# A macaron block on one core: quartered gate, down products by tokens, row statistics and additions moved to GpSimd

## The chip, the cores and the metric

One core of a Trainium2 chip runs the whole program. Its engines are TensorE (PE), VectorE (DVE), ScalarE (ACT), GpSimd (POOL) and SyncE (SP, which only issues DMAs). Times are device microseconds of one execution; a kernel's time is the median of its runs.

## The reference

For 4096 tokens x of 128 features (8 sequences of 512), all in float32 but the experts' products:

```python
x = x + 0.5 * ffn(layernorm(x))
x = x + attention(layernorm(x))   # one head, 4096 stored keys and values, softmax
x = x + 0.5 * ffn(layernorm(x))   # the same weights again

def ffn(x):                       # 8 experts of 176 hidden units, the best 2 of each token
    scores = sigmoid(x @ gate_w.T)
    _, sel = top_k(scores + expert_bias, 2)
    # routed: x * score in bfloat16, up, relu squared, down, summed over the two experts
    hs = square(relu(x @ shared_w_up.T))
    return routed + hs @ shared_w_down.T
```

## The kernel before

Tokens are handled in 8 groups of 512 (4 tiles of 128). `G` counts groups over both FFNs: 0 to 7 in the first, 8 to 15 in the second. Each engine has its own program, written out by hand; engines wait for one another on semaphores, and within an engine everything runs in the order written. So the order of calls in each `ffn(f)` is the schedule.

An FFN group goes like this. GpSimd computes the inverse deviation and normalises (L469, L483), TensorE transposes x to features by tokens (L1211), ScalarE copies it out of PSUM (L640) and GpSimd casts it to bfloat16 (L506). This runs three groups ahead. The gate (L1217) multiplies each tile of x, as the stationary operand, by the 8 columns of gate weights, so the logits stand by tokens. ScalarE takes exponentials (L648). `route_group(k, G)` (L973) is the routing of one group, or from group 2 on of two at once, in 16 small steps on VectorE: sigmoid, bias, twice a highest value with a tie broken by rank, sum of the two choices (k = 14), product with the score (k = 15). GpSimd spreads each weight over 16 rows (L495), TensorE transposes that (L1238) and ScalarE copies it (L671) to `wbc`, which holds for each hidden row and token the weight of its expert.

All experts are computed for all tokens: the hidden units, 8 x 176 = 1408, are 11 chunks of 128 rows. `up(G, k)` (L1255) makes two chunks (k = 5: one) of hidden rows by 512 tokens, VectorE multiplies relu by `wbc` (`relu_weighted`, L1028), ScalarE squares (L665), and `down(G, k)` (L1275) sums the chunks' products in one PSUM bank, features by tokens. The shared expert runs in float32: L1227 up, L656 relu, L660 square, L1289 down, added in the same bank. ScalarE copies the bank to `yT` (L676), TensorE transposes it back to tokens by features (L1247), and VectorE adds half of it to X (`residual`, L1043). The down products of slots 3 to 5 of a group are done within the next one.

```python
                    if i + 1 < GROUPS:
                        pe.wait_ge(xT_copied, min(n + AHEAD + 1, 2 * base + GROUPS))
                        if f == 0 and i + AHEAD >= GROUPS:
                            pe.wait_ge(xT_copied, GROUPS + 1)
                        transpose_weights(G + 1, xT_bank)
                    down(G, 1)
                    up(G, 4)
                    up(G, 5)
                    shared_down(G)
                    down(G, 2)
```

Layer norms are numbered n, 24 in all. For n from 4 to 8 VectorE takes only the raw statistics and GpSimd joins the halves of a row (`join_halves`, L447); for the others VectorE aggregates them (L914). During the first FFN GpSimd also splits the keys and values into two parts (L543 to L552). The attention lies between the FFNs; in its last steps it already normalises groups 8 to 10 and computes their gates (`early_gate`, L1480). SyncE stores each finished group (L428).

## Time and profile before

| | us |
|---|---|
| median of 3 runs (lowest to highest) | 642.77 (642.2 to 643.43) |
| the profiled execution | 644.01 |
| its span, first to last instruction | 642.2 |
| busy: TensorE, VectorE, ScalarE, GpSimd | 609.9, 531.3, 456.1, 398.9 |
| granted TensorE clock, mean over the span | 0.997 of 2.4 GHz |

The profile lists what each engine did. Busy time of matmuls is modelled: each one is shown until its result is out, and neighbours overlap, so the distance from start to start tells what one costs. "PEld" is the load of the stationary operand, which runs beside the products. The time slices tell where in the program the time lies: the first FFN ends at about 100 us, the second begins at 552.7.

### The profile page before, as it was taken

What the parts mean: (1) busy time and instruction counts of PE and PEld (TensorE: products, weight loads), DVE (VectorE), ACT (ScalarE), POOL (GpSimd) and SP (SyncE); (2) the same over time, 40 slices, a digit from 0 to 9 for tenths busy, and PEclk for the clock granted to TensorE, in tenths of its full rate; (3) what the DMA queues carried; (4) which work ended last, traced back from release to release, by engine and by line L of the source; (5) the groups of instructions that cost most, each with busy time, mean ns of one, the idle gap of its engine ahead of it and who ended that gap; (6) DMA issues with size and microseconds to landing.
All of it is one profiled execution on the core that took longest, in us unless ns stands there. A gap on an engine that the chain in (4) does not pass through costs nothing.

```text
span 642.2 us, 9438 instructions
## 1 busy us (share of the span) xinstructions
PE 609.9 (95%) x2884; PEld 430.1 (67%) x2884; DVE 531.3 (83%) x944; ACT 456.1 (71%) x765; POOL 398.9 (62%) x443
## 2 busy tenths in 40 slices
PE   7799999799999999999999999999999998999997
PEld 4455445567677787777777777777777766645543
DVE  5889887998987978978988897897898858699885
ACT  3577787566677767778777777777776775667886
POOL 4987770564486875966867777586687786524000
PEclk9899999999999999999999999999999999999999
DMA  8011210435447365374553835727355350000000
GB/s 313 6 57 42 65 34 1 114 74 131 113 96 170 73 152 113 85 173 91 132 126 79 177 85 126 152 59 178 82 121 130 77 123 1 2 17 17 34 33 33
DMA packets 36113, 59.19 MB, mean 92 GB/s; under 512 B 9312, under 2 KB 9952, under 8 KB 35936
## 3 DMA queue, kind: packets, MB, share of 16 engines
q1 hardware_dynamic: 31808, 52.82, 34.2%
q10 hardware_dynamic: 3744, 4.73, 2.9%
q0 software_dynamic: 512, 1.05, 0.6%
q8 instruction: 23, 0.38, 0.3%
q14 instruction: 26, 0.21, 0.1%
HBM read 8.23 MB, written 2.10 MB: 16 GB/s over the span
## 4 chain that ended last, share of the span: by engine, by line
PE 60%; DVE 24%; issue 5%; SPq 4%; ACT 3%; POOL 2%; DMA 1%; ACTq 0%; DVEq 0%; POOLq 0%
PE banks L1425 6%; PE banks L1427 6%; PE banks L1426 6%; PE banks L1466 6%; PE banks L1468 6%; PE banks L1467 6%; DVE bank_max L1143 6%; DVE E L1138 5%; PE banks L1281 4%; SPq L356 4%; PE banks L1272 4%; PE banks L1445 4%; DVE probsT L1039 4%; PE banks L1476 2%; DVE p_lo L1131 2%
## 5 line engine op out<-in xcount | busy, mean ns | idle before, releaser
L559 POOL TENSOR_TENSOR p_lo<-probsT,p_hi 128x768 fp32r<-128x768 f32 (+1 forms) x128 | 227.0, 1777 | 120.5 <-ACT p_hi L770 119.9
L1143 DVE TENSOR_REDUCE bank_max<-banks 128x1 f32<-128x1024 f32 x128 | 155.9, 1218 | 29.8 <-PE banks L1427 29.0
L770 ACT ACTIVATE p_hi<-probsT 128x768 fp32r<-128x768 f32 (+1 forms) x128 | 104.3, 816 | 27.7 <-PE banks L1468 22.8
L1425 PE MATMUL banks<-kv_lo,q_parts 128*128 128x512 f32 x256 | 111.5, 436 | 4.6 <-ACT E L795 1.7
L1138 DVE STREAM_TRANSPOSE E<-E 128x1024 f32<-128x1024 f32 x92 | 113.5, 1234 | 0.9 <-ACT E L795 0.9
L1039 DVE SCALAR_TENSOR_TENSOR probsT<-banks,E 128x1024 bf16<-128x1024 f32 x80 | 95.3, 1217 | 21.4 <-PE banks L1272 21.3
L669 ACT ACTIVATE probsT<-probsT 128x1024 bf16<-128x1024 bf16 x96 | 92.6, 982 | 23.2 <-DVE probsT L1039 18.7
L795 ACT ACTIVATE E<-banks,neg_max 128x1024 f32<-128x1024 f32 x92 | 102.4, 1113 | 8.6 <-DVE neg_max L1149 5.6
L1466 PE MATMUL banks<-p_hi,kv_lo 128*128 128x512 f32 x256 | 107.7, 421 | 0.3 <-issue 0.3
L1467 PE MATMUL banks<-p_lo,kv_hi 128*128 128x512 f32 x256 | 102.3, 400 | 0.0
L1468 PE MATMUL banks<-p_hi,kv_hi 128*128 128x512 f32 x256 | 102.2, 399 | 0.0
L1427 PE MATMUL banks<-kv_hi,q_parts 128*128 128x512 f32 x256 | 101.2, 396 | 0.0
L1426 PE MATMUL banks<-kv_hi,q_parts 128*128 128x512 f32 x256 | 101.1, 395 | 0.0
L754 ACT ACTIVATE p_hi<-banks 128x256 fp32r<-128x256 f32 (+1 forms) x128 | 52.2, 408 | 61.5 <-PE banks L1445 61.4
L1131 DVE TENSOR_TENSOR p_lo<-banks,p_hi 128x256 fp32r<-128x256 f32 (+1 forms) x128 | 56.1, 439 | 30.9 <-ACT p_hi L754 30.4
L1425 PEld LDWEIGHTS banks<-kv_lo,q_parts 128*128 128x128 f32 x256 | 48.2, 188 | 13.3 <-ACT E L795 3.1
L1466 PEld LDWEIGHTS banks<-p_hi,kv_lo 128*128 128x128 f32 x256 | 48.2, 188 | 12.5 <-issue 2.5
L1468 PEld LDWEIGHTS banks<-p_hi,kv_hi 128*128 128x128 f32 x256 | 48.1, 188 | 12.3
L1467 PEld LDWEIGHTS banks<-p_lo,kv_hi 128*128 128x128 f32 x256 | 48.2, 188 | 11.6 <-issue 1.7
L1427 PEld LDWEIGHTS banks<-kv_hi,q_parts 128*128 128x128 f32 x256 | 48.1, 188 | 11.2
L1272 PE MATMUL banks<-E,wup_b 128*128 128x512 bf16 x176 | 51.1, 384 | 4.3 <-DVE probsT L1039 3.0
L1445 PE MATMUL banks<-ident,probs 128*128 128x128 f32 x256 | 51.5, 276 | 3.3 <-DVE p_lo L1131 1.7
(132 smaller groups left out, 895.6 us busy)
## 6 DMA issues: line engine op xcount, KB each, us to landing
probsT<-E SPq DMA_DIRECT2D x208, 128.0 KB, 2.4
probsT<-E SPq DMA_DIRECT2D x232, 64.0 KB, 2.0
probsT<-E ACTq DMA_DIRECT2D x72, 64.0 KB, 2.3
E<-in_keys_values SPq DMA_DIRECT2D x8, 512.0 KB, 3.6
out<-X SPq DMA_DIRECT2D x8, 256.0 KB, 2.1
X<-in_x SPq DMA_DIRECT2D x1, 1280.0 KB, 8.8
probsT<-E POOLq DMA_DIRECT2D x16, 64.0 KB, 2.3
X<-in_x SPq DMA_DIRECT2D x3, 256.0 KB, 5.2
```

What stands on the lines that cost most here:

```text
L559: pool.tensor_tensor(moved_part(p_lo, ring), moved_pair(ring // UP, ring % UP), moved_part(p_hi, ring).bitcast(fp32), ALU.subtract).then_i ...
L770: act.activation(moved_part(p_hi, ring), moved_pair(ring // UP, ring % UP), ACT.Copy).then_inc(moved_hi_done, 1)
L795: act.activation(strips[:, 2 * h * QUADS:2 * (h + 1) * QUADS, :, :], source.rearrange("p k (c b q) -> p (k c) b q", b=QUADS, q=SQ), ACT.Ex ...
L1039: dve.scalar_tensor_tensor(hidden[:, k, :, :], up_banks[PAIR_BANK[k]], 0.0, spread.unsqueeze(1).to_broadcast([P, 2, N]), ALU.max, ALU.mult ...
L1138: dve.transpose(half, half).then_inc(squares_done, 1)
L1143: dve.tensor_reduce(bank_max[:, i % 2, h:h + 1], score_pair(u, i, h).rearrange("p b n -> p (b n)"), AX.X, ALU.max).then_inc(bank_max_done, 1)
L1425: pe.matmul(bank, qh, kl, start=True, stop=False)
L1426: pe.matmul(bank, ql, kh, start=False, stop=False)
L1427: pe.matmul(bank, qh, kh, start=False, stop=True).then_inc(scores_done, 1)
L1466: pe.matmul(OB, vl, hi, start=(c == 0), stop=False)
L1467: pe.matmul(OB, vh, lo, start=False, stop=False)
L1468: pe.matmul(OB, vh, hi, start=False, stop=(c == KC - 1)).then_inc(pv_done, 1)
```

## The change

- The gate's operands are swapped: the gate weights, padded to 32 columns, are stationary, and x moves. The four tiles go to the four column quarters of the array (`tile_position`), and the logits come out as rows 32t to 32t+7 by tokens. ScalarE takes exponentials of all 128 rows, and VectorE turns them with a transpose of 32x32 blocks before the routing. Tokens are thereby in another order, which the copy to `wbc` undoes.
- Routing: `STEPS` is 14; the last two operations are counted apart. In groups G + 1 = 2, 4, 6, 10, 12, 14 GpSimd does them, ahead of spreading the weights, and that stands before the row statistics now. On VectorE steps 0 to 5 stand in the even group (before: 0 to 8), 6 to 9 before `relu_weighted(G, 1)` and 10 to 13 behind it.
- Down and shared down: the hidden block is the stationary operand, 128 tokens at a time, and the weights move, so the result stands by tokens. `yT`, `copy_yT` and `transpose_back` go. Two result banks alternate.
- The transpose of the spread weights stands behind the shared down product.
- Second FFN: for n of 20 to 23 GpSimd joins the statistics; for groups 8 to 14 ScalarE copies half of the result to `half_result` and GpSimd adds it to X. Group 15 and the first FFN keep VectorE's addition, now straight from the result bank.

The core of the diff (declarations and semaphores that only follow are left out):

```diff
 RING = AHEAD + 1
-STEPS = 15
+STEPS = 14
 LOWEST = -3.0e38
...
 def joins_on_pool(n):
-    return AHEAD < n <= ATTENTION_LN
+    return AHEAD < n <= ATTENTION_LN or n > SECOND_LN + AHEAD
...
     return sum(not joins_on_pool(k) for k in range(n))
+def added_on_pool(G):
+    return GROUPS <= G < 2 * GROUPS - 1
+def added_before(G):
+    return sum(added_on_pool(k) for k in range(G))
...
         xT = [xq[:, :]] + [probs[:, 0, 0, c * N:(c + 1) * N] for c in range(AHEAD)]
+        expz_rows = probs[:, 0, 0, AHEAD * N:AHEAD * N + 2 * P].rearrange("p (s n) -> p s n", s=2)
+        expz = probs[:, 0, 0, AHEAD * N + 2 * P:].rearrange("p (s t e) -> p s t e", s=2, t=GT)
+        early_rows = wq_scaled[:, :]
         probsT = sb("probsT", [P, 2, MOVED * QUADS, KC, SQ], fp32)
...
         up_banks = [banks[:, 0:2, :], banks[:, 2:4, :]]
-        y_bank, z_bank, gate_bank, xT_bank = (banks[:, 4 + b, :] for b in range(4))
+        result_banks = [banks[:, 4 + b, :] for b in range(2)]
+        gate_bank, xT_bank = (banks[:, 6 + b, :] for b in range(2))
         TB, OB = banks[:, 2 * SCORE_PAIRS, :], banks[:, 2 * SCORE_PAIRS + 1, :]
...
+        def finishes_on_pool(G):
+            return G >= 2 and route_event(G) != route_event(GROUPS)
+        def routing(G):
+            T = GT * (2 if G >= 2 else 1)
+            return tuple(route[:, a, 0:T, :] for a in range(6))
         def wide_weights(G):
...
             for g in range(GROUPS):
-                sp.wait_ge(x_updated, GROUPS + g + 1)
+                if added_on_pool(GROUPS + g):
+                    sp.wait_ge(x_added, added_before(GROUPS + g + 1))
+                else:
+                    sp.wait_ge(x_updated, updated_before(2 * GROUPS))
                 sp.dma_start(out[:, tiles_of(g), :], X[:, tiles_of(g), :]).then_inc(stored, 16)
...
                 T = (slots.stop - slots.start) * GT
+                if finishes_on_pool(G):
+                    event = route_event(G)
+                    score, _, hit, _, first, second = routing(G)
+                    pool.wait_ge(route_step, STEPS * (event + 1))
+                    pool.tensor_tensor(hit, first, second, ALU.add).then_inc(route_summed, 1)
+                    pool.wait_ge(route_summed, event + 1)
+                    pool.wait_ge(weights_spread, event)
+                    pool.tensor_tensor(weight[:, slots, :, :].rearrange("p s t e -> p (s t) e"), hit, score, ALU.mult
+                                       ).then_inc(weights_ready, 1)
                 pool.wait_ge(weights_ready, route_event(G) + 1)
...
                                  .to_broadcast([P, T * E, ROWS])).then_inc(weights_spread, 1)
+            def add_result(G):
+                pool.wait_ge(result_copied, added_before(G + 1))
+                xg = X[:, tiles_of(G % GROUPS), :].rearrange("p t d -> p (t d)")
+                pool.tensor_tensor(xg, xg, half_result, ALU.add).then_inc(x_added, 1)
...
                     next_ln = i + AHEAD + 1
+                    if i % 2 == 1 and i + 1 < GROUPS:
+                        spread_weights(G + 1)
                     if next_ln < GROUPS + (1 - f):
...
                         spread_weights(1)
-                    if i % 2 == 1 and i + 1 < GROUPS:
-                        spread_weights(G + 1)
                     if i + AHEAD < GROUPS:
...
                         normalize(n + AHEAD + 1, next_ln % GROUPS)
+                    if i and added_on_pool(G - 1):
+                        add_result(G - 1)
                     if f == 0:
...
                 if G >= 2:
-                    act.wait_ge(route_step, STEPS * route_event(G - 2) + 1)
-                act.activation(expz[:, G % 2, :, :].rearrange("p t e -> p (t e)"), logits, ACT.Exp, scale=-1.0
-                               ).then_inc(expz_done, 1)
+                    act.wait_ge(expz_turned, route_event(G - 2) + 1)
+                act.activation(early_rows if G == GROUPS else expz_rows[:, G % 2, :], logits, ACT.Exp, scale=-1.0).then_inc(expz_done, 1)
...
                 wait(act, weighted, (G - 1) * SLOTS)
-                act.activation(wbc[:, G % 2, :], bank, ACT.Copy).then_inc(wbc_copied, 1)
-            def copy_yT(G):
+                act.activation(wbc[:, G % 2, :].rearrange("p (t a q) -> p t a q", t=GT, a=GT),
+                               bank.rearrange("p (a t q) -> p t a q", a=GT, t=GT), ACT.Copy).then_inc(wbc_copied, 1)
+            def copy_result(G):
                 act.wait_ge(down_done, (G + 1) * SLOTS)
-                wait(act, z_done, G)
-                act.activation(yT[:, :], y_bank[:, :], ACT.Copy).then_inc(yT_copied, 1)
+                wait(act, x_added, added_before(G))
+                act.activation(half_result, result_banks[G % 2], ACT.Copy, scale=0.5).then_inc(result_copied, 1)
...
                     cast_up()
-                    exp_logits(0, gate_bank[:, 0:GT * E])
+                    exp_logits(0, gate_bank[:, 0:P])
                     copy_xT(1, 1, 1, xT_bank)
                     cast_down()
-                    exp_logits(1, gate_bank[:, 0:GT * E])
+                    exp_logits(1, gate_bank[:, 0:P])
                     scale_q_weights()
...
                     if i + AHEAD < GROUPS:
-                        exp_logits(G + AHEAD, gate_bank[:, 0:GT * E])
+                        exp_logits(G + AHEAD, gate_bank[:, 0:P])
                     elif f == 0 and i + AHEAD == GROUPS:
...
                     square(G, 2)
+                    square(G, 3)
                     if i + 1 < GROUPS:
                         copy_wbc(G + 1, xT_bank)
-                    square(G, 3)
                 square(base + GROUPS - 1, PAIRS - 1)
                 square(base + GROUPS - 1, PAIRS)
-                copy_yT(base + GROUPS - 1)
...
                 T = (slots.stop - slots.start) * GT
-                score, biased, hit, tagged, first, second = (route[:, a, 0:T, :] for a in range(6))
+                score, biased, hit, tagged, first, second = routing(G)
                 top, first_tag, top2, second_tag = (best[:, a, 0:T] for a in range(4))
...
                 biases = ebias[:, :].unsqueeze(1).to_broadcast([P, T, E])
-                logits = expz[:, slots, :, :].rearrange("p s t e -> p (s t) e")
+                logits = expz[:, slots, :, 0:E].rearrange("p s t e -> p (s t) e")
                 weights = weight[:, slots, :, :].rearrange("p s t e -> p (s t) e")
...
                 if k == 0:
+                    dve.wait_ge(expz_done, G + (2 if T > GT else 1))
+                    wait(dve, route_step, STEPS * (event - 1) + 1)
+                    turned = expz[:, slots, :, :].rearrange("p s t e -> p (s t e)")
+                    if G == GROUPS:
+                        dve.transpose(turned[:, 0:P], early_rows)
+                        dve.transpose(turned[:, P:], expz_rows[:, 1, :]).then_inc(expz_turned, 1)
+                    else:
+                        dve.transpose(turned, expz_rows[:, slots, :].rearrange("p s n -> p (s n)")
+                                      ).then_inc(expz_turned, 1)
                     wait(dve, weights_ready, event)
-                    dve.wait_ge(expz_done, G + (2 if T > GT else 1))
-                else:
+                    dve.wait_ge(expz_turned, event + 1)
+                elif k <= STEPS:
                     dve.wait_ge(route_step, event * STEPS + k)
...
                 elif k == 14:
-                    dve.tensor_tensor(hit, first, second, ALU.add).then_inc(route_step, 1)
+                    dve.tensor_tensor(hit, first, second, ALU.add).then_inc(route_summed, 1)
                 else:
+                    dve.wait_ge(route_summed, event + 1)
                     wait(dve, weights_spread, event)
...
-                dve.wait_ge(z_done, G + 1)
+                dve.wait_ge(down_done, (G + 1) * SLOTS)
                 xg = X[:, tiles_of(g), :].rearrange("p t d -> p (t d)")
-                dve.scalar_tensor_tensor(xg, z_bank[:, :], 0.5, xg, ALU.mult, ALU.add).then_inc(x_updated, 1)
+                dve.scalar_tensor_tensor(xg, result_banks[G % 2], 0.5, xg, ALU.mult, ALU.add).then_inc(x_updated, 1)
...
                             dve.wait_ge(consts_set, 1)
-                            for k in range(STEPS + 1):
+                            for k in range(STEPS + 2):
                                 route_group(k, 0)
...
                     relu_weighted(G, 0)
+                    routes = i % 2 == 1 and i + 1 < GROUPS
+                    if routes:
+                        for k in range(6, 10):
+                            route_group(k, G + 1)
+                        relu_weighted(G, 1)
+                        for k in range(10, STEPS):
+                            route_group(k, G + 1)
                     if ahead < GROUPS + (1 - f):
                         moments_of(n + AHEAD + 1, ahead % GROUPS)
-                    if i % 2 == 1 and i + 1 < GROUPS:
-                        for k in range(9, STEPS + 1):
-                            route_group(k, G + 1)
                     if f == 0 and i == 0:
-                        for k in range(STEPS + 1):
+                        for k in range(STEPS + 2):
                             route_group(k, 1)
-                    relu_weighted(G, 1)
+                    if not routes:
+                        relu_weighted(G, 1)
                     relu_weighted(G, 2)
-                    if i:
+                    if i and not added_on_pool(G - 1):
                         residual(G - 1, i - 1)
...
                     if i % 2 == 0 and i + 2 < GROUPS:
-                        for k in range(0, 5):
+                        for k in range(0, 3):
                             route_group(k, G + 2)
...
                     if i % 2 == 0 and i + 2 < GROUPS:
-                        for k in range(5, 9):
+                        for k in range(3, 6):
                             route_group(k, G + 2)
...
+            def gate_products(bank, xt):
+                for t in range(GT):
+                    last = pe.matmul(bank[t * SQ:(t + 1) * SQ, :], gate_s[:, :], xt[:, t * P:(t + 1) * P], start=True,
+                                     stop=True, tile_position=(0, t * SQ))
+                last.then_inc(logits_done, 1)
             def gate(n, G):
...
                 wait(pe, weighted, (G - AHEAD) * SLOTS)
-                for t in range(GT):
-                    last = pe.matmul(gate_bank[:, t * E:(t + 1) * E], xT[G % RING][:, t * P:(t + 1) * P], gate_s[:, :],
-                                     start=True, stop=True)
-                last.then_inc(logits_done, 1)
+                gate_products(gate_bank[:, 0:P], xT[G % RING])
...
                 last.then_inc(wbc_done, 1)
-            def transpose_back(G):
-                pe.wait_ge(yT_copied, G + 1)
-                wait(pe, x_updated, G)
-                for t in range(GT):
-                    last = pe.transpose(z_bank[:, t * D:(t + 1) * D], yT[:, t * P:(t + 1) * P], ident[:, :])
-                last.then_inc(z_done, 1)
...
                 if k == 0:
-                    wait(pe, yT_copied, G)
+                    if G >= 2 and added_on_pool(G - 2):
+                        pe.wait_ge(result_copied, added_before(G - 1))
+                    elif G >= 2:
+                        pe.wait_ge(x_updated, updated_before(G - 1))
                 chunks = (2 * k,) if k == PAIRS else (2 * k, 2 * k + 1)
                 for c in chunks:
-                    last = pe.matmul(y_bank[:, :], wdown_b[:, c, :], hidden[:, k, c % 2, :], start=(c == 0),
-                                     stop=(c == CH - 1))
+                    for t in range(GT):
+                        last = pe.matmul(result_banks[G % 2][:, t * D:(t + 1) * D],
+                                         hidden[:, k, c % 2, t * P:(t + 1) * P], wdown_b[:, c, :],
+                                         start=(c == 0 and t == 0), stop=(c == CH - 1 and t == GT - 1))
                 last.then_inc(down_done, 1)
...
-                pe.matmul(z_bank[:, 0:columns], ident[:, :], ones[:, 0:columns], start=True, stop=True)
+                pe.matmul(result_banks[1][:, 0:columns], ident[:, :], ones[:, 0:columns], start=True, stop=True)
...
                 pe.wait_ge(hs_done, G + 1)
-                pe.matmul(y_bank[:, :], sdown_s[:, 0, :], hs[:, 0:N], start=False, stop=False)
-                for c in range(2):
-                    pe.matmul(y_bank[:, c * HALF:(c + 1) * HALF], sdown_s[:, 1 + c, :], hs[:, N:], start=False,
+                for t in range(GT):
+                    tokens = result_banks[G % 2][:, t * D:(t + 1) * D]
+                    pe.matmul(tokens, hs[:, t * P:(t + 1) * P], sdown_s[:, 0, :], start=False, stop=False)
+                    at_column = N + t * P % HALF
+                    pe.matmul(tokens, hs[:, at_column:at_column + P], sdown_s[:, 1 + t * P // HALF, :], start=False,
                               stop=False)
...
                         up(G, 2)
-                        if i:
-                            transpose_back(G - 1)
                         down(G, 0)
...
                         up(G, 3)
+                    down(G, 1)
+                    up(G, 4)
+                    up(G, 5)
+                    shared_down(G)
                     if i + 1 < GROUPS:
...
                         transpose_weights(G + 1, xT_bank)
-                    down(G, 1)
-                    up(G, 4)
-                    up(G, 5)
-                    shared_down(G)
                     down(G, 2)
...
                     scores(0, 1, 0)
-                transpose_back(base + GROUPS - 1)
```

## Rows read from the trace of the kernel before

**Rows 1.** The page: busy time by engine, and the chain by engine.
```profile
PE 609.9 (95%) x2884; PEld 430.1 (67%) x2884; DVE 531.3 (83%) x944; ACT 456.1 (71%) x765; POOL 398.9 (62%) x443
...
PE 60%; DVE 24%; issue 5%; SPq 4%; ACT 3%; POOL 2%; DMA 1%; ACTq 0%; DVEq 0%; POOLq 0%
```

**Rows 2.** Time slices, one per group: busy us by engine, granted clock, DMA share, GB/s.
```profile
33.90:44.20 10.30, 10.30 (x55) 5.86 (x54) 9.37 (x20) 8.87 (x13) 7.97 (x18) 1.00 0.16 51
...
54.80:66.70 11.90, 11.05 (x55) 6.08 (x56) 10.87 (x24) 9.86 (x14) 8.11 (x18) 1.00 0.15 44
...
564.00:575.90 11.90, 10.95 (x55) 6.06 (x56) 11.12 (x29) 9.56 (x14) 4.68 (x9) 1.00 0.06 23
575.90:586.20 10.30, 10.30 (x55) 5.92 (x54) 9.17 (x23) 7.83 (x12) 3.70 (x8) 1.00 0.07 27
...
627.50:642.20 14.70, 10.17 (x44) 4.29 (x42) 7.52 (x8) 8.59 (x11) 0.00 (x0) 0.99 0.09 36
```

**Rows 3.** Timeline of TensorE, group 10: start, length of the run, line, count.
```profile
575.87 1.02 PE L1230 MATMUL banks<-probs,sup_s 128*128 128x512 f32 x2
576.82 0.65 PE L1233 MATMUL banks<-probs,sup_s 128*64 128x256 f32 x4
577.40 0.82 PE L1281 MATMUL banks<-probsT,wdown_b 128*128 128x512 bf16 x3
...
579.36 0.60 PE L1252 MATMUL banks<-ident,probsT 128*128 128x128 f32 x4
...
580.34 1.06 PE L1223 MATMUL banks<-gate_s,probs 128*128 128x8 f32 x8
581.26 0.59 PE L1272 MATMUL banks<-E,wup_b 128*128 128x512 bf16 x2
...
583.20 1.02 PE L1291 MATMUL banks<-probsT,sdown_s 128*128 128x512 f32 x2
584.06 1.03 PE L1294 MATMUL banks<-probsT,sdown_s 128*128 128x256 f32 x4
```

**Rows 4.** Weight loads and short pairs: line L1281, two loads in a timeline, a run of L1476.
```profile
L1281 PEld LDWEIGHTS banks<-probsT,wdown_b x176: 95/98/151, 23.8 to 637.2; 128*128 128x128 bf16 x176
...
577.40 0.11 PEld L1281 LDWEIGHTS banks<-probsT,wdown_b 128*128 128x128 bf16 x2 [0.39 <-issue]
...
555.11 1.05 PE L1476 MATMUL banks<-wo_s,attended 128*128 128x128 f32 x8
```

**Rows 5.** Waits, 33.9 to 99.2 us, then 564 to 642.2 us: total, times, longest.
```profile
DVE probsT L1039 <- PE banks L1272: 6.7, 9, 1.8
...
DVE probsT L1039 <- PE banks L1272: 8.4, 10, 1.8
```

**Rows 6.** VectorE: line L1138, and groups of instructions from 564 to 607.9 us.
```profile
L1138 DVE STREAM_TRANSPOSE E<-E x92: 1224/1234/1248, 114.9 to 510.3; 128x1024 f32<-128x1024 f32 x92
...
L1047 DVE SCALAR_TENSOR_TENSOR X<-banks,X 128x512 f32<-128x512 f32 x4 | 2.7, 681 | 0.0
...
L921 DVE BATCH_NORM_AGGREGATE moments<-stats 128x2 f32<-128x6 f32 x12 | 1.1, 156 | 0.1
```

**Rows 7.** GpSimd's addition L580 by itself; a routing step on VectorE beside GpSimd's work.
```profile
L580 POOL TENSOR_TENSOR X<-X,attended x14: 1269/1288/1296, 180.3 to 536.9; 128x512 f32<-128x512 f32 x14
...
543.45 1.26 DVE L1022 TENSOR_TENSOR route<-route 128x64 f32<-128x64 f32 x1
```

**Rows 8.** Group 0: timelines of TensorE and VectorE with idle time, and a time slice.
```profile
27.84 1.09 PE L1244 MATMUL banks<-ident,probsT 128*128 128x128 f32 x4 [1.54 <-issue]
...
30.67 1.23 DVE L1039 SCALAR_TENSOR_TENSOR probsT<-banks,E 128x1024 bf16<-128x1024 f32 x1 [1.37 <-PE banks L1272]
...
28.00:29.00 1.00, 1.00 (x5) 0.81 (x5) 0.90 (x4) 0.04 (x1) 1.00 (x3) 0.50 0.00 0
```

**Rows 9.** The end: timeline of ScalarE's last copy and VectorE's last addition.
```profile
637.66 0.60 ACT L679 ACTIVATE probsT<-banks 128x512 f32<-128x512 f32 x1 [0.48 <-PE banks L1281]
...
639.00 0.69 DVE L1047 SCALAR_TENSOR_TENSOR X<-banks,X 128x512 f32<-128x512 f32 x1 [2.84 <-PE banks L1252]
```

39 lines of the change are left out of this document (19 added, 20 removed).

## The prediction

> **What bounds the kernel now.** I read the page first. TensorE is busy 95% of the span and the chain that ended last runs 60% through it, 24% through VectorE [rows 1]. Matmul ends are modelled, so I then took the time slices from one group of 512 tokens to the next, cut where the shared product of each group starts [rows 2]. In both FFNs a group without the second half of the routing takes about 10.3 us, one with it 11.9 us. In the first kind TensorE has no gap; in the second VectorE is busy 10.9 to 11.1 of 11.9 us and TensorE idles nearly 1 us. The attention between the FFNs (some 100 to 550 us) is not edited, apart from three gate products at its end. So the time is to be won in 16 groups, at the start and at the tail.
>
> The TensorE timeline of one group [rows 3] gives the price list, by start to start: down product with 512 moving columns 0.216 us; transposing back 4 tiles 0.43 (4 x 0.109); gate 580.34 to 581.26 = 0.92; shared down product 0.86 for L1291 (583.20 to 584.06) and as much for L1294. The waits [rows 5] say that the two engines hold each other up by turns: VectorE waited 6.7 us for up products in the first FFN and 8.4 us in the second.
>
> **The change, part by part.**
>
> *Down products by tokens.* The hidden block becomes the stationary operand, 128 tokens at a time, so 11 pairs of load and product with 512 columns become 44 pairs with 128. Before: 11 x 0.216 = 2.37 us. The unknown is the spacing p of a bf16 pair with 128 columns; no such pair is in the trace. Lower bound: a quarter of a 512-column product, 0.054 us. Upper bound: the fp32 pair with 128 columns, 0.111 us ((1.05 - 0.275)/7 in the row of L1476 [rows 4]), where the 0.19 us load counts. The bf16 load is recorded at 0.098 us and two of them start about 0.013 us apart (0.11 - 0.098) [rows 4]; the product that needs the load starts right behind it. A load that another can follow after 0.013 us should hide behind 0.054 us of columns, so I take p = 0.056: 44 x 0.056 = 2.46, **+0.09 us** a group. The range keeps 0.054 to 0.111.
>
> *Shared down product by tokens.* 16 fp32 pairs with 128 columns at 0.111 = 1.78 instead of 2 x 0.86 = 1.72: **+0.06**.
>
> *Transposing back.* It goes: **-0.43** on TensorE. ScalarE's copy before it (0.60 us, L679 [rows 9]) goes in the first FFN and stays as copy_result in the second, but is no longer on TensorE's way, since two result banks alternate.
>
> *Quartered gate.* 32 stationary columns per tile, four tiles in the four column quarters of the array, logits by rows. The nearest row is the half product L1233: two tiles of 256 columns [rows 3]. It starts 0.95 us after L1230, whose two passes take 0.85, so 0.10 to change over; and it gives way after 0.58 where its columns alone need 0.43 if the halves run together, so 0.15 to change back. For the gate: 0.10 + 0.21 + 0.15 = 0.46, **-0.45** after rounding. If the quarters don't run together: 0.25 + 4 x 0.21 = 1.1, +0.18.
>
> TensorE's sum: 0.09 + 0.06 - 0.43 - 0.45 = **-0.73 us** for a group with a gate, **-0.28** without one.
>
> *VectorE.* Each routing now transposes the exponentials first: the 128x1024 transpose takes 1.23 us [rows 6], a quarter of it about 0.31, with issue 0.35 per pair of groups. In the first FFN nothing is taken off in return but two closing steps of 0.23 of each later routing. So there a pair of groups is -0.1 us for VectorE, no gain. In the second FFN seven residual additions of 0.68 go to GpSimd, and four aggregations (1.1 us over three groups, with the memset 0.4 each) [rows 6]: 4.8 + 1.6 = 6.4 us off. The order "6 to 9, relu, 10 to 13" only moves steps, it puts relu and weighting of slot 1 ahead of four of them: nothing, or a little gain for ScalarE's next square.
>
> *GpSimd.* It takes 7 additions of the form of L580, 1.29 us each [rows 7], the joins and two small operations per routing, in a stretch where it is idle over half the time [rows 2]. They hide; if they don't, the stores are late, and only the last one is on the path, whose addition VectorE does. Two waits are new on its queue. Spreading the weights now stands ahead of the statistics and waits for VectorE's steps up to 13 with one relu between them, about 1.2 + 1.0 + 1.2 + 1.0 = 4.4 us into the group; behind it stand join, cast, normalisation and the key conversion. All of that was 8.1 us in such a group [rows 2], plus 0.5 for the two new operations: 13.0, and the normalised x is transposed some 2.5 us into the next group, at 14. It fits, in the first FFN by 1 us only, so there GpSimd is the next to be late.
>
> *ScalarE.* Eight copies of 0.60 less in the first FFN, exponentials over 128x128 instead of 128x32, a regrouped copy of the weights. Off the path. In the second FFN copy_result waits until GpSimd has added the result before; behind that wait stand all squares of the group, and so the down products. The addition before was due a whole group earlier, so I cost the wait at nothing. TensorE's first down product waits for the result of two groups ago where it waited for the copy of one: looser.
>
> *Moved weights transpose.* It now stands behind the shared down product. At the start this matters: TensorE stood still for 1.54 us before L1244 in group 0, in the slice that follows the granted clock is 0.50 (the 1.2 GHz level) against 1.00 elsewhere, and VectorE then waited 1.37 us for an up product [rows 8]. With the transpose behind them, slots 4 and 5 and the shared product fill that hole. I count VectorE's 1.37 and some of what the lower clock cost: **-1.7**. Elsewhere the weights are needed 2 to 3 us later than they are ready: nothing.
>
> *Tail.* Before, the last down product is followed by copy (637.66), transposes and the addition at 639.00 [rows 9]. The addition can now start at 637.66: **-1.35**.
>
> **The sum.** First FFN: the start -1.7; four intervals in which TensorE has no gap, three at 0.73 and the last without gate at 0.28, -2.5; two with VectorE as the limit, -0.2 each, -0.4; the last transposing back, -0.4: together -5.0. Second FFN: first group -0.3; two intervals with routing, where TensorE gives 0.73 and VectorE over 0.9, -0.8 each; two without, -0.73 each; two late ones without gate, -0.35 each; the last group -0.28 and the tail -1.35: together -5.7. Gates at the end of attention: three times 0.45, half of it in waits, -0.7. Total **-11.4 us**. The profiled execution took 644.0 us (span 642.2): 632.6. The median of the runs is 642.8, 1.2 lower, so I forecast **631.4**.
>
> **The rivals.**
>
> *Pairs bound by the load* (slower than before). Place: the 44 pairs of each group, 704 in all, on an engine without gaps. Each 0.010 us more costs 7 us. The gain of 11.4 is used up at p = 0.056 + 11.4/704 = 0.072. At the fp32 spacing of 0.111 it would be +39 - 11 = +27, about 670. For it speaks that every 128-column pair in the trace runs at 0.108 to 0.112; against it that those are fp32 loads of 0.14 to 0.19 us, and bf16 loads follow one another after 0.013. Chance 0.09.
> The Trainium skill, "TensorE: Matmul & The Clock Gate", section "Back-to-back issue gap", speaks against the change here: it has a sustained stream of load and product pairs at about 81 ns for 128 columns and about 131 ns for 512. By it the sum would be an estimated 704 x 0.025 = 17.6 us worse, some 649. The trace contradicts its second figure, since pairs with 512 columns stand at 216 ns here, and the same section gives an isolated gap of about 56 ns; so I give it a part of the 0.09.
>
> *VectorE becomes the limit and keeps most of it.* In the first FFN it already fills 10.9 of 11.9 us in every second group, and if the other groups only hand their 0.73 over to longer waits of TensorE, what is left is start, tail and the second FFN in part: -1.7 - 1.35 - 3 = -6, about 637. Added to it can be contention: a routing step of 0.23 us took 1.26 beside GpSimd's work (L1022 at 543.45) [rows 7]; with GpSimd's additions in three routings that is up to 3 us. Chance 0.15.
> The Trainium skill, "SBUF — State Buffer", section "Who interferes with whom", has the reason: an operation of VectorE with two inputs in SBUF and one of GpSimd that reads SBUF exclude each other for a whole instruction. The trace agrees with that row.
>
> *The quarters don't run together.* Then 0.63 is missing in some nine groups that TensorE bounds, about 5.5 us: 637. Against it: the two halves of L1233 do. Chance 0.06.
>
> *More than forecast.* VectorE's waits for up products (6.7 and 8.4 us [rows 5]) shrink with TensorE's time in the groups with routing too, and square follows relu sooner. Then 0.5 more in each of six groups and 1 to 2 at the start: 627. Chance 0.15.
>
> **The numbers.** The forecast has 0.55, from 629 to 634. What a measurement of this kernel can tell from no change is about 0.2%, 1.3 us. All cases but the first end below that: faster 0.87, with 0.04 within 0.2% for a p near 0.072 or for several small losses together, slower 0.09. The range for 8 in 10 reaches from 626 to 638: it takes in both cases around 637 and the one at 627, and leaves the loads out.
>
> **What would show it.** Pairs of down products in the changed trace at 0.056 us start to start (at 0.08 or more the forecast is wrong); the gate in about 0.46 us with its four tiles starting nearly together; groups in the second FFN of 9.6 us without routing and about 11 with; in the first FFN 9.6 and 11.7; no stop of 1.5 us before the first weights transpose, and a granted clock without a slice at 0.50 or with a shorter one; the last addition right behind the last down product. It would be wrong in its mechanism if TensorE now waits for VectorE for longer than it gained, or if attention changes by more than 1 us.

## The result, and the profile after

The changed kernel takes 640.2 us (median of 7 runs, 638.77 to 641.1), the kernel before 643.75 in the same session (7 runs). The ratio is 0.9941, 95% interval 0.9922 to 0.9961: 3.8 us faster, a third of the 11.4 that were forecast, and outside the range. The profiled execution is the median one: 640.2, span 638.4 against 642.2.

The page after, busy time by engine (compare [rows 1]):

```profile
PE 597.5 (94%) x3508; PEld 443.3 (69%) x3508; DVE 525.7 (82%) x915; ACT 455.0 (71%) x756; POOL 414.7 (65%) x482
```

TensorE lost 12.4 us of busy time and VectorE 5.6, but the span only 3.8. Where it went is seen by cutting both traces at the same places: the shared up product of group 0, of 7, of 8 and of 15. Time slices of the kernel before (columns as in [rows 2]):

```profile
16.70:98.80 82.10, 76.28 (x372) 41.20 (x371) 71.29 (x143) 60.49 (x84) 64.43 (x125) 0.98 0.13 39
98.80:553.10 454.30, 439.23 (x2072) 338.82 (x2071) 378.75 (x610) 323.05 (x583) 309.17 (x253) 1.00 0.47 107
553.10:627.50 74.40, 71.21 (x356) 38.78 (x356) 65.02 (x137) 58.44 (x81) 18.44 (x36) 1.00 0.06 22
```

and of the changed one, which has the last group as well (before: 14.70 [rows 2]):

```profile
16.90:97.50 80.60, 71.15 (x640) 47.47 (x638) 71.49 (x141) 58.77 (x77) 66.20 (x131) 1.00 0.13 41
97.50:551.00 453.50, 437.64 (x2118) 338.20 (x2116) 377.41 (x612) 322.67 (x582) 308.84 (x253) 1.00 0.45 107
551.00:625.30 74.30, 68.27 (x625) 46.24 (x624) 60.85 (x108) 59.49 (x80) 31.72 (x68) 1.00 0.06 23
625.30:638.40 13.10, 8.96 (x90) 6.14 (x87) 6.95 (x7) 8.39 (x11) 1.27 (x1) 1.00 0.11 40
```

Groups 0 to 6 gave 1.5 us, the last group of the first FFN with the attention 0.8, the last group with the tail 1.6; the second FFN's groups 8 to 14 gave 0.1, though TensorE lost 2.9 us of work there and VectorE 4.2. Slices by group (those of [rows 2], but for the last):

```profile
31.70:42.90 11.20, 9.88 (x97) 6.79 (x95) 10.44 (x22) 8.46 (x12) 7.95 (x19) 1.00 0.16 48
52.90:65.20 12.30, 10.29 (x97) 6.88 (x94) 11.47 (x24) 9.05 (x12) 8.96 (x20) 1.00 0.14 44
561.70:573.10 11.40, 10.09 (x94) 6.79 (x94) 9.97 (x23) 9.43 (x13) 5.60 (x15) 1.00 0.01 2
573.10:583.30 10.20, 9.87 (x96) 6.67 (x93) 8.51 (x14) 8.06 (x12) 7.82 (x17) 1.00 0.14 54
```

Group by group, from the start of one shared up product to that of the next, in us (the forecast is the prediction's sum, spread over its groups; groups 1, 3, 5, 9, 11 and 13 hold the second half of a routing; groups 7 and 15 end in the stretches above):

| group | before | forecast change | after | measured change |
|---|---|---|---|---|
| 0 | 17.21 | -1.7 | 14.83 | -2.38 |
| 1 | 10.35 | -0.73 | 11.22 | +0.87 |
| 2 | 10.60 | -0.73 | 9.95 | -0.65 |
| 3 | 11.81 | -0.2 | 12.30 | +0.49 |
| 4 | 10.60 | -0.73 | 9.94 | -0.66 |
| 5 | 12.13 | -0.2 | 12.42 | +0.29 |
| 6 | 9.40 | -0.28 | 9.92 | +0.52 |
| 8 | 10.92 | -0.3 | 10.65 | -0.27 |
| 9 | 11.82 | -0.8 | 11.42 | -0.40 |
| 10 | 10.35 | -0.73 | 10.24 | -0.11 |
| 11 | 11.37 | -0.8 | 11.42 | +0.05 |
| 12 | 10.35 | -0.73 | 10.18 | -0.17 |
| 13 | 10.19 | -0.35 | 10.43 | +0.24 |
| 14 | 9.39 | -0.35 | 9.92 | +0.53 |

So groups 1 to 6 together are 0.9 us slower than before, where 2.9 faster were forecast. But that sum hides two opposite things: groups 2 and 4 gave nearly all that was forecast for them, and the groups beside them took it back.

TensorE's timeline of group 10 (compare [rows 3]) shows that the prices were right:

```profile
573.10 1.08 PE L1296 MATMUL banks<-probs,sup_s 128*128 128x512 f32 x2
...
574.69 0.84 PE L1345 MATMUL banks<-wdown_b,probsT 128*128 128x128 bf16 x12
575.37 0.59 PE L1330 MATMUL banks<-E,wup_b 128*128 128x512 bf16 x2
...
577.17 0.62 PE L1345 MATMUL banks<-wdown_b,probsT 128*128 128x128 bf16 x8 [0.34 <-ACT probsT L716]
577.72 0.43 PE L1282 MATMUL banks<-probs,gate_s 128*32 128x128 f32 x8
578.08 0.61 PE L1330 MATMUL banks<-E,wup_b 128*128 128x512 bf16 x2
...
579.73 0.38 PE L1358 MATMUL banks<-sdown_s,probsT 128*128 128x128 f32 x2
...
581.51 0.60 PE L1310 MATMUL banks<-ident,probsT 128*128 128x128 f32 x4
581.95 0.61 PE L1345 MATMUL banks<-wdown_b,probsT 128*128 128x128 bf16 x8
582.39 0.59 PE L1330 MATMUL banks<-E,wup_b 128*128 128x512 bf16 x2
```

Twelve down pairs take 0.68 us (574.69 to 575.37) and eight 0.44 (581.95 to 582.39): 0.056 a pair. The quartered gate takes 0.36 (577.72 to 578.08), the shared down product 1.78 (579.73 to 581.51). What has grown is the wait in brackets, of TensorE for the square. In the kernel before it came to 1.6 us in the first FFN (33.9 to 99.2 us) and in the second (564 to 642.2 us) to:

```profile
PEld banks L1281 <- ACT probsT L669: 4.5, 10, 0.7
```

In the changed kernel, first from 31.7 to 97.5 us, then from 561.7 to 638.4:

```profile
PEld banks L1345 <- ACT probsT L716: 7.4, 14, 1.0
...
DVE probsT L1096 <- PE banks L1330: 7.1, 7, 1.9
```

```profile
DVE probsT L1096 <- PE banks L1330: 12.9, 11, 1.9
...
PEld banks L1345 <- ACT probsT L716: 10.9, 15, 1.3
```

VectorE's waits for up products, 6.7 and 8.4 us before [rows 5], grew too. Both engines have less to do and each waits more for the other.

The tail did what was forecast. Timelines of TensorE and VectorE:

```profile
633.79 1.39 PE L1345 MATMUL banks<-wdown_b,probsT 128*128 128x128 bf16 x22
```

```profile
635.22 0.69 DVE L1104 SCALAR_TENSOR_TENSOR X<-banks,X 128x512 f32<-128x512 f32 x1 [1.74 <-PE banks L1345]
```

The addition follows the last down product directly; before, copy and transposes stood between [rows 9].

### The profile page after: what moved, and what is told of

Same layout as the page of the kernel before. It is cut to its first block, busy times and chain, and to the rows that moved or that the text cites. A ratio compares the mean times of both kernels' runs of the same rounds, so it can differ in the third digit from the quotient of the medians.

```text
span 638.4 us, 10666 instructions
## 1 busy us (share of the span) xinstructions
PE 597.5 (94%) x3508; PEld 443.3 (69%) x3508; DVE 525.7 (82%) x915; ACT 455.0 (71%) x756; POOL 414.7 (65%) x482
## 3 DMA queue, kind: packets, MB, share of 16 engines
q0 software_dynamic: 512, 1.05, 0.6%
## 4 chain that ended last, share of the span: by engine, by line
PE 65%; DVE 24%; issue 4%; ACT 3%; SPq 1%; DMA 1%; POOL 1%; ACTq 0%; DVEq 0%; POOLq 0%
PE banks L1488 8%; PE banks L1489 7%; PE banks L1490 7%; PE banks L1529 7%; PE banks L1531 7%; PE banks L1530 7%; DVE probsT L1096 6%; PE banks L1508 4%; DVE bank_max L1205 4%; PE banks L1345 4%; DVE E L1200 3%; PE banks L1330 3%; PE banks L1539 2%; PE banks L1361 2%; PE banks L1358 2%
## 5 line engine op out<-in xcount | busy, mean ns | idle before, releaser
L716 ACT ACTIVATE probsT<-probsT 128x1024 bf16<-128x1024 bf16 x96 | 92.4, 981 | 16.7 <-DVE probsT L1096 12.4
L1345 PEld LDWEIGHTS banks<-wdown_b,probsT 128*128 128x128 bf16 x704 | 42.5, 98 | 30.8 <-ACT probsT L716 21.7
L1345 PE MATMUL banks<-wdown_b,probsT 128*128 128x128 bf16 x704 | 52.8, 220 | 7.9 <-ACT probsT L716 7.9
```

What stands on the lines that cost most here:

```text
L1345: last = pe.matmul(result_banks[G % 2][:, t * D:(t + 1) * D], hidden[:, k, c % 2, t * P:(t + 1) * P], wdown_b[:, c, :], start=(c == 0 and ...
```

## The experiments

Every run was timed together with the kernel before, in one session. "Interiors" are the profiled distances from the shared up product of group 0 to that of 7, and of 8 to 15. Between two profiles of similar kernels the stretch between (attention) differs by up to 2 us, so I read the interiors for mechanisms and the ratio for the total. A group that an edit doesn't touch mostly repeats from profile to profile within 0.05 us.

| run | median us | ratio (95% interval) | interiors |
|---|---|---|---|
| before | 643.75 | | 82.1, 74.4 |
| the change | 640.2 | 0.9941 (0.9922 to 0.9961) | 80.6, 74.3 |
| e1_weights_before_up4 | 640.61 | 0.9952 (0.994 to 0.9963) | 80.6, 75.2 |
| e2_up1_first | 639.71 | 0.9938 (0.9926 to 0.995) | 80.1, 75.1 |
| e3_weights_and_up1 | 640.18 | 0.9946 (0.9934 to 0.9958) | 79.9, 75.8 |
| e7_gate_as_before | 639.82 | 0.994 (0.9925 to 0.9956) | 79.1, 74.5 |
| e5_vector_adds | 639.1 | 0.9938 (0.9923 to 0.9953) | 80.5, 73.5 |
| e4_before_weights_late | 654.57 | 1.017 (1.0152 to 1.0188) | 86.1, 81.6 |
| e4b_..._square_first | 648.24 | 1.0068 (1.0045 to 1.0092) | 82.4, 79.4 |
| g0_before_first_late | 644.0 | 0.9999 (0.999 to 1.0008) | 80.2, 74.4 |
| i1_first_early | 641.55 | 0.9977 (0.9964 to 0.999) | 81.5, 74.2 |
| f2_routing_and_weights_as_before | 650.09 | 1.011 (1.0082 to 1.0137) | 85.3, 77.1 |
| f3_split_as_before_weights_early | 642.63 | 0.9981 (0.9972 to 0.9991) | 83.0, 74.0 |
| h1_less_shared_down | 635.51 | 0.9874 (0.9862 to 0.9887) | 79.7, 72.9 |
| h2_less_vector | 637.19 | 0.9901 (0.9887 to 0.9916) | 79.6, 72.0 |
| h3_both_less | 630.12 | 0.9798 (0.9785 to 0.9811) | 76.9, 69.3 |
| i2_early_where_ready | 639.21 | 0.9933 (0.9921 to 0.9944) | 80.1, 73.8 |
| i3_..._vector_adds | 638.14 | 0.9918 (0.9906 to 0.9931) | 80.1, 73.0 |
| j1_best | 638.28 | 0.9914 (0.9897 to 0.9931) | 80.4, 73.0 |

### Is TensorE's work still the bound? The gate put back

The changed kernel with the old gate (tiles of x stationary, 0.92 us instead of 0.45). There the exponentials of group 8 stand in a part of the attention's buffer for exponentials that is still in use, so a part of the attention's result is overwritten; the work is the same.

```diff
-                    last = pe.matmul(bank[t * SQ:(t + 1) * SQ, :], gate_s[:, :], xt[:, t * P:(t + 1) * P], start=True,
-                                     stop=True, tile_position=(0, t * SQ))
+                    last = pe.matmul(bank[:, t * E:(t + 1) * E], xt[:, t * P:(t + 1) * P], gate_s[:, 0:E], start=True,
+                                     stop=True)
```

> The changed kernel with the gate as before: x stationary, eight moving columns, exponentials over 128x32, no transpose of them on VectorE. TensorE has 0.47 us more for each gate again. Loop theory: the gate stands where TensorE is ahead of VectorE, so its saving was never on the path, while the transpose of the exponentials on VectorE (0.44 us) is, in each pair of groups: 0 to 2.5 us less than the changed kernel. Theory of the prediction, TensorE without gaps in the groups without routing: 4 us or more slower than the changed kernel.

In total nothing changed: 639.82, ratio 0.994. But the edit does two things at once. TensorE has 0.47 us more per gate, and VectorE is rid of the transpose of the exponentials (0.44 us per routing). By group they come apart. A slice of group 10, which took 10.24 us in the changed kernel:

```profile
571.60:582.10 10.50, 10.17 (x96) 7.54 (x94) 8.41 (x14) 8.38 (x13) 7.77 (x17) 1.00 0.14 52
```

Groups 10 and 12 are 0.30 and 0.36 us longer with the old gate, so there most of the gate's saving had arrived; groups 3, 5, 8 and 11 are 0.2 to 0.35 us shorter. Group 0 is 0.9 us shorter but starts 0.9 us later (17.75 against 16.89). So the quartered gate together with the transpose that it needs was worth nothing; its saving on TensorE by itself was worth something in two groups, and for groups 2 and 4, unchanged within 0.05 us, this run can't part the two.

### Who keeps the square late in the second FFN? VectorE's additions back

```diff
 def added_on_pool(G):
-    return GROUPS <= G < 2 * GROUPS - 1
+    return False
...
```

> The changed kernel with VectorE's additions in the second FFN too (no result copies on ScalarE, no additions on GpSimd). Loop theory: of two additions of 0.68 us one lies in VectorE's stretch of the loop and the other where VectorE is ahead; against it a routing step that took 0.90 instead of 0.19 us beside GpSimd's addition is short again. Within 1 us of the changed kernel. Theory of the prediction, VectorE limits by its sum: 0.68 us more in each of seven groups, 4 to 5 us slower. Theory of ScalarE's queue: 1 to 2 us faster, as the square of slot 0 no longer stands behind the copy.

Seven additions of 0.68 us came back to VectorE, and by the ratio the time is the same (0.9938 against 0.9941); the second interior is 73.5 instead of 74.3. So giving the additions away, with the copy on ScalarE that this needs, gained nothing, and the copy costs. The ScalarE timeline of the changed kernel, group 10:

```profile
574.80 0.81 ACT L705 ACTIVATE probsT<-banks 128x768 f32<-128x768 f32 x1 [0.77 <-PE banks L1299]
575.57 0.60 ACT L728 ACTIVATE probsT<-banks 128x512 f32<-128x512 f32 x1
576.07 1.05 ACT L716 ACTIVATE probsT<-probsT 128x1024 bf16<-128x1024 bf16 x1
```

The shared relu (L705) waits for the shared up product, then comes copy_result (L728), then the first square (L716), and TensorE's down product starts at 577.17, 4.07 us after the shared up product. Before, the distance was much the same, 3.99 us, but TensorE's own work filled it, transposing back last (from 575.87 to 579.86, with transposing back at 579.36 [rows 3]). Taking 0.43 us of that work away leaves the chain as long as it was. Without the copy (the run with VectorE's additions, ScalarE and then TensorE) the square follows the relu and the down product comes 3.57 us after its shared up product at 572.44; groups 10 and 12 are 0.29 and 0.23 us shorter for it:

```profile
574.15 0.81 ACT L705 ACTIVATE probsT<-banks 128x768 f32<-128x768 f32 x1 [0.77 <-PE banks L1299]
574.86 1.05 ACT L716 ACTIVATE probsT<-probsT 128x1024 bf16<-128x1024 bf16 x1
```

```profile
572.44 1.08 PE L1296 MATMUL banks<-probs,sup_s 128*128 128x512 f32 x2
...
576.01 0.61 PE L1345 MATMUL banks<-wdown_b,probsT 128*128 128x128 bf16 x8
```

### Is it the hand-over between the engines? Order on TensorE

Three orders of the changed kernel: the weights transpose ahead of the up product of slot 4, where TensorE waits 1.05 us in groups with routing; the up product of slot 1 ahead of the last two down products of the group before; and both. In groups 0 and 8 the transpose stays where it is. The edit in short, without its waits:

```diff
 down(G, 1)
+transpose_weights(G + 1, xT_bank)      # e1, e3
 up(G, 4)
 up(G, 5)
 shared_down(G)
-transpose_weights(G + 1, xT_bank)
```

> The changed kernel, with the transpose of the spread weights between the first half of the down products and up(G, 4) instead of behind the shared down product (group 0 keeps it). Same work, another place. Theory of the hand-over: the interior of the FFNs gained nothing because what stands on TensorE between up(G, 5) and up(G+1, 0), up(G+1, 1) is what VectorE waits for at every group's start (0.56 to 1.16 us before slot 0, 1.15 to 1.93 before slot 1), and the change put 0.44 us of weights transpose exactly there. Then VectorE's idle time before slot 0 or 1 falls by about 0.4 us in some eight groups, and the time by 2.5 to 3.5 us against the changed kernel (to 0.989 to 0.990 of the kernel before). Theory that the two engines are filled with work, or that later routing weights set the pace: no change within 0.5 us, or slower by up to 1.5 us because TensorE then stands before up(G, 4) until the weights are there.

> The changed kernel, with up(G, 1) ahead of the last two down products of the group before (0.67 us of TensorE) instead of behind them. Same work. Hand-over theory: VectorE's wait before slot 1 (1.15 us in the even groups, 1.93 in the late ones) shrinks by about 0.6 us in seven groups: 3 to 4.5 us less than the changed kernel. Work theory: nothing. A third theory, ScalarE's squares as the limit: slower, as the result of the group before is taken off later and the square of slot 0 stands behind that in the second FFN.

> Both moves of the two kernels above together. Hand-over theory: the gains add up as long as VectorE has idle time before slots 0 and 1: 5.5 to 8 us less than the changed kernel, about 633 us where the changed kernel takes 640. If another chain (square, GpSimd) follows closely, clearly less than the sum of both.

None gained (ratios 0.9952, 0.9938, 0.9946). The first order fails by what is ready when. GpSimd and TensorE in group 11 of the changed kernel:

```profile
588.68 0.33 POOL L535 TENSOR_TENSOR route<-route 128x64 f32<-128x64 f32 x1 [7.42 <-DVE route L1045]
...
589.47 1.04 POOL L543 COPY probsT<-weight 128x1024 f32<-128x1024 f32 x1
```

```profile
590.56 0.82 PE L1330 MATMUL banks<-E,wup_b 128*128 128x512 bf16 x3 [1.05 <-DVE probsT L1096]
```

The weights are spread at 590.51, just when slot 2 sets the up product free, so the transpose can't use that hole; and it made group 13 longer (11.3 against 10.4 us): there TensorE stood 1.14 us ahead of the transpose, and the up product of slot 4 went out behind it.

### The late transpose by itself, and the start

The kernel before, with nothing but the transpose behind the shared down product; then the same with the square of slot 3 ahead of the copy to `wbc`, as the change has it; then only in groups 0 and 8; and last the changed kernel with these two groups as before.

```diff
-transpose_weights(G + 1, xT_bank)
 down(G, 1)
 up(G, 4)
 up(G, 5)
 shared_down(G)
+transpose_weights(G + 1, xT_bank)
 down(G, 2)
```

> The kernel before, with only the place of the weights transpose changed as the change does it: behind the shared down product. Hand-over theory: the start gains 1.5 to 2.4 us (the hole before the first transpose and the half clock behind it go), and groups that VectorE then waits for at their start lose 0.4 us each, seven to ten of them: 3 to 4 us lost, in all 1 to 2 us slower than the kernel before or the same. If the place doesn't matter in the interior: 1.5 to 2.4 us faster.

> The kernel before, with the weights transpose behind the shared down product and, as in the change, ScalarE's copy of the weights behind the square of slot 3 instead of ahead of it. The kernel that moved the transpose alone lost 10.9 us, its groups ending in a wait of 0.93 us for that square. Theory: 2.2 us gained at the start, 0.44 us lost in each group whose transpose stands in the loop, nine or so: 1 to 3 us slower than the kernel before. If the loss of the first kernel was the place of the transpose and not the square behind the copy: still some 10 us slower.

Alone, the move costs 10.9 us (1.017). ScalarE's copy waits for the transpose, and the square of slot 3 stands behind it. ScalarE, then TensorE's down product of slot 3:

```profile
591.16 0.60 ACT L674 ACTIVATE E<-banks 128x512 f32<-128x512 f32 x1 [2.13 <-PE banks L1244]
...
591.66 1.99 ACT L669 ACTIVATE probsT<-probsT 128x1024 bf16<-128x1024 bf16 x2
...
592.76 0.60 PE L1281 MATMUL banks<-probsT,wdown_b 128*128 128x512 bf16 x2 [0.77 <-ACT probsT L669]
```

With the square first 6.6 us of that return; the rest (1.0068) lies mostly in groups with routing, two of which hold a stretch at half clock in the profile (shown at the end). Of each of the two kernels all executions but one had a mean granted clock below 1.00. The two exceptions took 652.68 us and, with the square first, 644.85, where the kernel before took 642.37 to 643.35 at 1.00 in the session of the latter. So at full clock too most of the loss, some 8 us, is the square's, and 1.5 to 2.5 us remain, by one execution each. The order of the square is a needed part of the change, and the late transpose brings nothing in the steady groups and may cost.

> The kernel before with one edit: in the first group of each FFN alone the transpose of the weights stands behind the shared down product, as the change puts it in all. Theory: the 1.54 us hole in group 0 and the half clock behind it go and nothing else changes, so 2.0 to 2.6 us off the kernel before (641.3 against 643.6, ratio 0.9964), which is most of what the whole change gained. Rival, the start gained through the down products and the gate: under 0.7 us.

> The changed kernel with one edit: in the first group of each FFN the transpose of the weights is back behind the up product of slot 3 (late in all others). Reading of the changed kernel's trace: group 0 gets its hole back and perhaps a stretch at half clock, 1.3 to 2.4 us slower than the changed kernel. Rival, by the run that moved it alone in the kernel before (no gain, ratio 0.9999): the same time within 0.6 us, the start was never on the path by itself.

In the kernel before the start alone gave nothing (0.9999), though groups 0 to 6 are 1.9 us shorter in its profile. In that execution a stretch at half clock stands ahead of group 0 instead of inside it, group 0 starts 1.1 us later (17.8 against 16.7), and the attention's stretch is 0.7 us longer:

```profile
10.90:14.30 3.40, 3.40 (x6) 1.32 (x6) 2.64 (x12) 0.25 (x2) 2.83 (x6) 0.50 0.99 413
```

In the changed kernel the same step, undone, costs 0.36% or 2.3 us. Its trace has the hole again, 1.47 us on TensorE, but no half clock behind it:

```profile
27.89 0.63 PE L1310 MATMUL banks<-ident,probsT 128*128 128x128 f32 x4 [1.47 <-issue]
```

```profile
28.00:31.50 3.50, 3.50 (x36) 3.22 (x36) 3.25 (x9) 2.72 (x4) 3.41 (x7) 1.00 0.00 0
```

Group 0 is 1.0 us longer there, and nothing else differs in the FFNs. So the hole costs 1.0 and does not always bring the half clock. The other 1.3 in the medians is seen in the mean granted clock of each execution. Six of eleven executions of this kernel had 0.999 or 1.00, with a median of 640.75 us, 0.9 above that of the changed kernel's six at 1.00 (639.83); the other five had 0.995 to 0.997 and a median of 642.91. Of the changed kernel only one of seven lay so low. So in the median such an execution is 2.2 us longer; whether the hole makes them more frequent, eleven and seven executions can't tell. In the kernel before, the step gives nothing at full clock either: four executions at 1.00 took 642.74 to 643.51 us, two without the step 642.57 and 643.43. Why, stays open.

### The routing's order

The changed kernel with routing and spreading in the old order and the transpose at its old place (groups 0 and 8 late); then only VectorE's split of the steps as before, with GpSimd's spreading first.

```diff
-                        for k in range(6, 10):
-                            route_group(k, G + 1)
-                        relu_weighted(G, 1)
-                        for k in range(10, STEPS):
-                            route_group(k, G + 1)
+                        for k in range(9, STEPS):
+                            route_group(k, G + 1)
```

> The changed kernel, with the order of the routing steps on VectorE, of spreading on GpSimd and of the weights transpose on TensorE as before (the first group of each FFN keeps its transpose late; gate, down products, results and GpSimd's operations as in the changed kernel). Theory of the loop, formed after the first runs: two groups take as long as one turn of VectorE's stretch from slot 1 of the even group to slot 2 of the odd one, and TensorE's from up(G, 4) there to up(G+1, 1). In the changed kernel the weights are ready only when slot 2 is, so their transpose (0.44 us) stands in the loop wherever it is put behind that; moving it ahead of up(G, 4) alone changed nothing. With the old order they are ready while TensorE waits anyway. So 0.44 us less in each of six routing groups and in the last two without routing: 2.5 to 3.5 us less than the changed kernel. Rival, that portioned routing itself was a gain: slower than the changed kernel by 1 us or more.

> The changed kernel, with three things put otherwise: the routing's steps split as in the kernel before (0 to 4 and 5 to 8 in the even group, 9 to 13 in the odd one, all right behind slot 0 and ahead of the statistics and of slot 1), the spreading first on GpSimd as the change has it, and the transpose of the weights back behind the up product of slot 3, where TensorE waits for the first square (groups 0 and 8 keep the late place). Loop theory: the last step 13 is done some 2.5 us into the odd group, the weights are spread at 4.5 to 5, when TensorE would wait anyway, and 0.44 us leaves TensorE's unbroken stretch in 14 groups; VectorE's work in its stretch stays. So 0.4 off each of some eight to ten groups, 3 to 4 us off the changed kernel, about 636.5. Rival, the weights come later than TensorE gets there (as in the run where routing and spreading order were both undone): a wait ahead of the transpose in six groups, 1 us each, slower than the changed kernel by up to 4.

Both are slower than the change: 650.09 and 642.63. All executions of the first had a mean granted clock of 0.987 to 0.997, and its profile has a stretch at half clock in group 1, so a part of its loss is that. In the first GpSimd joins statistics (from 594.23) before it finishes the weights, and TensorE stands still ahead of the transpose. GpSimd, then TensorE:

```profile
597.56 1.04 POOL L543 COPY probsT<-weight 128x1024 f32<-128x1024 f32 x1
```

```profile
598.70 0.63 PE L1305 MATMUL banks<-ident,probsT 128*128 128x128 f32 x4 [1.61 <-issue]
```

The second run, with the statistics behind the routing on VectorE and behind the spreading on GpSimd, takes 7.5 us less than the first. So with the joins and the two closing steps on GpSimd, routing and spreading must stand ahead of the statistics. In the second the weights were in time and TensorE's wait moved to the even groups, where nine steps instead of six now stand ahead of slots 4 and 5 on VectorE:

```profile
56.03 1.12 PE L1292 MATMUL banks<-probs,sup_s 128*128 128x512 f32 x2 [1.75 <-DVE probsT L1096]
```

### Cuts on either engine

Three runs that leave work out of the changed kernel: half of the shared down product in groups 1, 3, 5, 9, 11, 13 (TensorE, 6 x 0.9 = 5.4 us); steps 9 to 13 of five routings (VectorE, 5.8 us); both.

```diff
-                    pe.matmul(tokens, hs[:, at_column:at_column + P], sdown_s[:, 1 + t * P // HALF, :], start=False,
-                              stop=False)
+                    if G % 2 == 0 or G % GROUPS == GROUPS - 1:
+                        pe.matmul(tokens, hs[:, at_column:at_column + P], sdown_s[:, 1 + t * P // HALF, :],
+                                  start=False, stop=False)
...
+                short = G >= 4 and G != GROUPS
+                if short and 9 <= k < STEPS:
+                    return
...
-                                             ).then_inc(route_step, 1)
+                                             ).then_inc(route_step, 6 if short else 1)
```

> The changed kernel; in the six groups with the second half of a routing (1, 3, 5, 9, 11, 13) half of the shared down product is left out: 4 of 8 fp32 pairs, 0.9 us of TensorE in each, 5.4 us in all (the output lacks that part of the shared expert). It lies in the stretch in which TensorE never stops, between the up product of slot 4 and the next group's first ones. Loop theory (two groups take one turn: an unbroken stretch of VectorE, then an unbroken one of TensorE): what is cut there comes off the time, 4 to 5.4 us against the changed kernel, so about 635 us, ratio to before near 0.987. Rival, VectorE alone bounds the pair of groups: less than 1.5 us, and TensorE's waits grow by what was cut, as they did for the quartered gate. Rival, TensorE's total work counts: 5.4 as well, so this run parts the first rival from the other two and the run with less VectorE work parts these.

> The changed kernel with five routing steps of VectorE left out (9 to 13, the choice of the second expert) in the routings of groups 4, 6, 10, 12 and 14: 5 x 0.23 = 1.15 us in each of groups 3, 5, 9, 11, 13, 5.8 us in all (these groups keep the second expert of the routing before). Loop theory: 4 to 5.8 us off the changed kernel, about 635 us, since VectorE's stretch is the other half of the turn. Rival, TensorE's total work is the bound: under 1 us. Rival, VectorE alone: 5.8. If this run and the one with the halved shared product both gain nearly all of what was cut, the two engines' stretches stand in series; if each gains about half, they overlap and hold each other up by turns.

> The changed kernel with both cuts at once: half of the shared down product left out in groups 1, 3, 5, 9, 11 and 13 (5.4 us of TensorE) and five routing steps left out in groups 3, 5, 9, 11 and 13 (5.8 us of VectorE); these parts of the shared expert and of the second expert's choice are missing. Alone they took 2.3 and 3.3 us off the interiors of the FFNs (from the shared up product of group 0 to that of 7, and of 8 to 15). Turns theory: the sum or more, 5.6 to 9 us off the changed kernel's interiors, since what one cut turned into waits of its engine is now used by the other; total near 633 or below. Rival, a third limit (ScalarE's squares, GpSimd's spreading) lies right behind: 4 us or less, no more than the better of the two and a little.

Interiors of the three, in this order:

```profile
16.50:96.20 79.70, 67.17 (x604) 44.67 (x614) 73.04 (x141) 58.37 (x77) 66.30 (x131) 1.00 0.14 42
548.20:621.10 72.90, 64.74 (x590) 43.51 (x599) 61.26 (x108) 59.50 (x80) 31.73 (x68) 1.00 0.06 23
```

```profile
16.80:96.40 79.60, 69.75 (x628) 47.42 (x638) 69.80 (x131) 58.63 (x77) 66.19 (x131) 1.00 0.13 41
549.10:621.10 72.00, 67.25 (x615) 46.20 (x623) 58.10 (x93) 58.91 (x80) 31.72 (x68) 1.00 0.06 23
```

```profile
17.10:94.00 76.90, 68.32 (x615) 44.68 (x614) 69.54 (x131) 58.30 (x77) 66.12 (x131) 1.00 0.14 42
545.70:615.00 69.30, 65.43 (x600) 43.51 (x599) 58.06 (x93) 58.90 (x80) 31.70 (x68) 1.00 0.07 24
```

Against the changed kernel's 80.6 and 74.3, TensorE's cut gave 0.9 + 1.4 = 2.3 of 5.4 us, VectorE's 1.0 + 2.3 = 3.3 of 5.8, and both together 3.7 + 5.0 = 8.7 of 11.2, more than the sum of 5.6. So neither engine bounds the groups alone, and a third limit takes at most 2.5 of the 11.2 us. They pass the work to and fro. TensorE's cut by group shows how: groups 1 and 13 gave all of their 0.9 us, groups 3 and 5 none, and groups 9 and 11 gave 0.9 of which the next ones, 10 and 12, took back 0.9 and 0.45. By the ratios the three are 0.67, 0.40 and 1.43% below the changed kernel, or 4.3, 2.6 and 9.2 us. They agree that both cuts together give more than the sum, but not in the sizes: the three profiles have 1.0 to 1.9 us less in the attention's stretch, which no edit touches, and nothing explains that. The shares by engine are read from the interiors.

### A better version

The transpose stays late only where the weights are not ready: in groups 2, 4, 6, 10, 12 and 14 it goes back behind the up product of slot 3. Then VectorE's additions with it, and last the up product of slot 1 first in the first FFN.

> The changed kernel with the transpose of the weights at its old place in groups 2, 4, 6, 10, 12 and 14 only, where the next group's weights were spread a group earlier and TensorE waits for squares just then. Turns theory: 0.3 to 0.44 off groups 6, 13 or 14 as seen in the run with routing and weights as before, and something under half of it in the others, since it only leaves TensorE's side: 0.6 to 1.5 us in all against the changed kernel, about 639.2. Rival: it only fills a wait on one side and pushes slot 4's product back on the other, nothing.

> As the run before it, and the additions of the second FFN done by VectorE from the result banks instead of ScalarE's copy and GpSimd's addition. By themselves the VectorE additions took nothing to 1 us off the changed kernel. Expected: the two add up to 1 to 2 us off, about 638.5, the best of the correct versions; rival: each uses the same slack and together they give what one gives.

> The changed kernel with three edits: the weights transpose at its old place in the even groups (all but 0 and 8), the additions of the second FFN by VectorE, and in the first FFN alone the up product of slot 1 ahead of the last two down products of the group before. If the parts add up: another 1.0 to 1.3 us off the version without the third edit, about 637. Rival, in the first FFN both edits use the same slack of TensorE: no more than 0.5 us off that version, about 638.

In the profile 0.43 us came off group 6, 0.32 off group 14, 0.1 off group 12 and nothing off the three others (interiors 80.1 and 73.8, 0.9 us less in all); the ratio, 0.9933, can't be told from the changed kernel's 0.9941. With the additions the second interior is 73.0, and groups 10 and 12 take 9.68 us, 0.67 less than in the kernel before. TensorE has no gap in them. A slice of group 10:

```profile
572.40:582.00 9.60, 9.60 (x96) 6.84 (x93) 8.28 (x15) 7.54 (x11) 5.28 (x15) 1.00 0.08 30
```

This is the group that was forecast: neither edit alone gives it (10.24 and 9.95 us in group 10). At 638.14 us the second of them is 5.3 us faster than the kernel before (0.9918) and 1.5 faster than the change by the ratios; the intervals of the two (0.9906 to 0.9931, 0.9922 to 0.9961) overlap a little. The third edit added nothing (0.9914).

## Why the prediction was wrong, and where it was right

*TensorE's prices: right.* The down pair stands at 0.056 us as taken, the shared down product at 1.78 for 1.78, the gate at 0.36 plus 0.10 to change over for 0.46. The rival of pairs bound by the load is out, and so is that of quarters that don't run together, by its 1.1 us. The sum was 0.73 less per group, and TensorE's busy time in the two interiors fell by 5.1 and 2.9 us.

*"Four intervals in which TensorE has no gap, three at 0.73", and the same in the second FFN: this step failed.* It was priced at 2.9 us in groups 1 to 6 and some 4.1 in groups 8 to 14, and lost 0.9 in the first and gained 0.1 in the second. A TensorE without gaps is the last to arrive, but it doesn't follow that it is late by as much as is taken off. The step multiplied TensorE's saving by the number of groups, and priced at nothing what the change puts in the way elsewhere. The table by group and the runs show where it went:

- Groups 2 and 4 gave 0.65 us each of the 0.73. Groups 3 and 5 beside them grew by 0.5 and 0.3. For each pair VectorE had as much work as before (20.0 and 19.9 us busy before, 20.1 and 20.0 after), and the pairs of 22.41 and 22.73 us became 22.25 and 22.36. The forecast had added TensorE's 0.73 in one group to 0.2 in the next, though it counted no gain for VectorE in the pair.
- Group 1 was counted as bound by TensorE ([rows 2], 10.3 us), but it holds a routing: VectorE was busy 9.4 us of it before and 10.5 after, and it grew by 0.9. In groups 1 and 3 TensorE now waits 1.1 us for VectorE ahead of the up product of slot 4. On VectorE a routing step more stands there, and some steps are slower than before. That this is the cause is read from the traces and was not tried by itself; with the old split of the steps, groups 2 and 4 grew instead, to 11.5 us.
- In groups 10 and 12 transposing back stood ahead of the down product of slot 0. There the chain shared up, shared relu, copy, square took 4.07 us, no less than before, so the down product could not come sooner. Without the copy, and with the weights transpose back at its old place, the groups take 9.68 us: 0.67 of the 0.73 arrives.
- Groups 6, 13 and 14 grew by 0.5, 0.2 and 0.5 us. In 6 and 14 putting the transpose back gives 0.43 and 0.32 of it.

The cuts show the same for whole pairs of groups: in the interiors one engine's saving alone gives 40 to 60%.

*"Elsewhere the weights are needed 2 to 3 us later than they are ready: nothing": wrong.* The late transpose costs. It lies in the stretch of TensorE from the up product of slot 4 to the next group's slot 0, for which VectorE waits (12.9 us in the second FFN), while its old place had a wait of TensorE beside it. In the kernel before it cost 0.7% even with the square ahead of the copy (a part of that at half clock); in the changed one, putting it back in six groups saved 0.9 us of the interiors, too little for the ratio to show.

*VectorE, second FFN, "6.4 us off": a part was taken off, and the additions brought nothing.* Its busy time fell by 4.2 us in groups 8 to 14. Of the rest a part went to contention: the first routing step took 0.90 us beside GpSimd's addition of 1.28, where it takes 0.20 in the run without that addition. What giving the statistics to GpSimd brought was not tried. Timelines of VectorE and GpSimd after:

```profile
580.40 0.90 DVE L1064 TENSOR_SCALAR route<-probs 128x64 f32<-128x64 f32 x1
```

```profile
579.97 1.28 POOL L551 TENSOR_TENSOR X<-X,probsT 128x512 f32<-128x512 f32 x1
```

The second rival had named this, and with its first half (TensorE's gain handed over to waits, about 637) it came nearest: a gain of 6 us where 3.8 came, as it counted 3 us in the second FFN. It should have held the first place.

*copy_result "cost at nothing": wrong.* Not the wait for GpSimd's addition that I looked at, but the 0.5 us of the copy itself ahead of the first square sets the down product back: without it groups 10 and 12 are 0.29 and 0.23 us shorter.

*The start, -1.7:* group 0 gained 2.4 us in the profile, of which group 1 took back 0.9. The step is worth 2.3 us in the medians of the changed kernel and nothing in the kernel before, so the size was plausible and the reason only in part: the hole is worth 1.0, and the half clock is not tied to it.

*Attention, -0.7 for the early gates and -0.4 for the last transposing back:* -0.8 measured, which is within the 2 us by which this stretch differs between similar kernels, so it confirms neither. The run with the old gates has the stretch as short, so no share of theirs is seen. From the last down product of group 7 to the shared up product of group 8 the kernels that transpose back need 441.1 to 442.8 us, those that don't 439.0 to 441.4; the two ranges touch, and that it is the transposing back was not tried by itself.

*The last group and the tail, -0.28 and -1.35:* -1.6, right. *GpSimd hides its new work:* right, given the new order.

## What to carry to other kernels

Where two engines hand tiles to each other and both are 80 to 92% busy, a saving counts only on the chain that is late at that spot: for each removed piece, ask what the next consumer waits for, with the time of its whole chain, before multiplying the saving by the number of groups. A cheap test is to leave work out on one engine, then on the other, then on both; if both give more than the sum, balance the two rather than speed up one. And a move that costs nothing on its own engine can stand ahead of another engine's queue: the copy behind the moved transpose held a square, and with it 6.6 of the 10.9 us that the move cost. A saving that seems lost may only be covered: it showed in groups 10 and 12 once both things ahead of it were gone.

## What the runs showed of the hardware beyond what was expected

- Pairs of load and product with 128 bf16 columns run at 0.056 us over 22 pairs in a row, so the load, recorded at 0.098 us, hides behind its neighbours: a pair costs 0.056 us where a quarter of a 512-column product is 0.054. The figure of 81 ns in the Trainium skill, "TensorE: Matmul & The Clock Gate", section "Back-to-back issue gap", does not hold here.
- The quartered gate is eight passes of 128 columns (four fp32 products, two passes each) and takes 0.36 us with the change back; one behind the other they would take 0.88 at the 0.11 of [rows 4], hardly less than the old gate's 0.92. So the quarters do run together, and that is what it saves.
- Stretches at half clock (1.2 GHz) came at different places in kernels that hardly differ: once at 27.5 us in the profile of the kernel before, nowhere in that of the changed one, twice in one run of the late transpose, shown here, and not behind every hole:

```profile
572.20:575.60 3.40, 3.40 (x8) 1.68 (x6) 2.87 (x4) 2.19 (x4) 0.52 (x2) 0.50 0.21 80
596.10:599.50 3.40, 3.40 (x7) 1.73 (x6) 2.82 (x3) 2.14 (x4) 0.47 (x2) 0.50 0.20 77
```
